# A two-layer model on eight cores: rows of the light FFN turned by DMA in the first stage, and q and k projected ahead of it in the first block

## The chip, the cores and the metric

The kernel runs on one Trainium2 chip, on all 8 cores. Each core computes one batch element on its own; the cores exchange no data. A time is the device time in microseconds (us) of the slowest of the eight cores. A profile shows one execution, on its slowest core (core 4 here), and times in it count from the start of the span.

## The reference

For one batch element x is 2048 tokens by 1024 channels. Two layers run in sequence, each `x = x + s * silu(f)` with an attention part s and a feed-forward part f of the normalised rows. The change touches only the start of the first layer:

```python
xn = _layernorm(x)                                   # rows of 1024 channels
x_proj = silu(xn @ W1 + b1); u, v, q, k = split(x_proj, 4)
scores = einsum('bqhd,bkhd->bhqk', qh, kh); attn = silu(scores) / S
y = _layernorm(attn_v * u) @ W2 + b2                 # attention part of layer 0
# feed-forward part of layer 0, on xn: rmsnorm, a light FFN for every row,
light = gelu(rmsnorm(xn) @ w1_l.T + b1_l) @ w2_l.T + b2_l
# and a heavy FFN for the 1024 rows with the highest scores xn . routing_token
```

Layer 1 is an attention with softmax and a gated FFN with 4096 hidden channels; its matmuls are most of the time.

## The kernel before

The program is written engine by engine: each helper appends an instruction to the list of one engine (`Q["t"]` TensorE, `Q["s"]` ScalarE, `Q["v"]` VectorE, `Q["g"]` POOL, `Q["y"]` SP), with waits on counters between them. Each engine runs its list in order, so the order in which the Python code calls the helpers is the order on each engine. DMAs are issued by SP (`y_dma`) or by POOL (`g_dma`); SP's waits stand in SP's list like any other entry, so a DMA is not issued before the waits of all DMAs ahead of it are met.

The first stage runs over 16 tiles of 128 rows (tile `tt`), in 4 blocks of 4 tiles (block `bl` holds tiles 4 bl to 4 bl + 3). It loads a tile of x (`xt0`, six buffers, lines 257 to 263) and then does this:

- `stats(bl)` (line 335): VectorE computes mean and variance of the four tiles (lines 343 to 346), ScalarE one square root, VectorE a few 128x4 operations, the last of them at line 363.
- `scale_rows(tt)` (line 365): `xnb`, the rows normalised for the attention (by ScalarE at line 373 for the first four tiles, by POOL at line 378 for the rest; two buffers), and `xrb`, the rows normalised for the FFN (POOL, line 383; four buffers). SP stores xrb to `xrsp` in HBM, for the later gather of the heavy rows.
- `turn_rows(tt, ...)` (line 390): TensorE turns xnb (eight 128x128 transposes into a PSUM bank, line 398) and VectorE copies the bank to `xn` (line 402); TensorE turns xrb (line 409) and ScalarE copies that bank to `xrT` (line 413); VectorE multiplies the rows with the routing token `rtb`, which is loaded once, and sums them (line 419); then SP loads the tile six further on.
- `light1(bl, m)` (line 425): the first matmul group of the light FFN, four groups of eight 128x512 matmuls on `xrT` and `w1l`, and a gelu on ScalarE. xrT has one buffer for a block; a new block writes it after light1 of the block before. `w1l` is made once by VectorE from the loaded `w1lf` (`fold_w1l`, line 280).
- `proj_uqk` (line 284) and `proj_v2` (line 302): projections q, k, u (eight 128x512 matmuls each) and v (two groups) of the block, with silu on ScalarE.

In the loop over the blocks, `stats` of the next block and `scale_rows` of its first two tiles come first; then light1 of this block, then q, k, u, v, v, and behind each of the first four of these one tile of the next block is turned. When the stage is done on TensorE, POOL issues the load of the next projection weights (`ld_wu[1]`), and the attention of layer 0 begins.

Of the kernel before, what the change touches and what calls it, by code (L numbers as in the profile page):

```python
# [17 lines left out]
NCH = 8  # L18
# [13 lines left out]
def build_program():  # L32
# [75 lines left out]
    Q = {"t": [], "s": [], "v": [], "g": [], "y": []}  # L108
# [40 lines left out]
    def SI(emit): return _inc("s", cs, emit)  # L149
# [32 lines left out]
    vrs = lambda nm, a, b: VROW[0:1, VR[nm] + a:VR[nm] + b]  # L182
# [6 lines left out]
    eye_bf = small("eye_bf", [128, 128], BF16)  # L189
# [67 lines left out]
    def load_x0(tt):  # L257
        if tt < NTT:
            sl = tt % NX
            if x0_free[sl] is not None:  # L260
                wk("y", *x0_free[sl])
            x0_ld[tt] = y_dma(qx0[sl], xt0[sl][:], xtok[tt * 128:(tt + 1) * 128, :])
    for tt in range(4):
        load_x0(tt)
    k_rt = y_dma(stream("qrt"), rtb[:], vrs("rt", 0, 1024).partition_broadcast(128))
    w1lv = w1lT.rearrange("(c p) n -> p c n", p=128)
    qw1l = [stream("qw1l0"), stream("qw1l1")]
    ld_w1l = [y_dma(qw1l[0], w1lf[0][:], w1lv[:, 0:4, :])]
    for tt in range(4, NX):
        load_x0(tt)  # L270
    ld_w1l.append(y_dma(qw1l[1], w1lf[1][:], w1lv[:, 4:8, :]))

    wk("g", x0_ld[3])
    ld_wu[0] = g_dma(qwu[0], wuqk[0][:], Wuqk[0, :, :, :])
# [115 lines left out]
    def turn_rows(tt, k_n, k_r, st):  # L390

        sl = tt % NX
        s2 = tt % 2
        s4 = tt % 4
        b = take()
        wk("t", k_n)
        for c in range(NCH):
            (TN if c < NCH - 1 else TI)(lambda t, c=c, b=b, s2=s2: t.transpose(
                pbh(b)[:, c * 128:(c + 1) * 128], xnb[s2][:, c * 128:(c + 1) * 128], eye_bf[:]))
        xnb_free[s2] = tok(ct)  # L400
        wk("v", tok(ct))
        VI(lambda v, tt=tt, b=b: v.tensor_copy(
            xn[:, :, tt * 128:(tt + 1) * 128], pbh(b).rearrange("p (c n) -> p c n", c=NCH)))
        give(b, tok(cv))
        k_xn[tt // 4] = tok(cv)
        b = take()
        wk("t", k_r)
        for c in range(NCH):
            (TN if c < NCH - 1 else TI)(lambda t, c=c, b=b, s4=s4: t.transpose(
                pbh(b)[:, c * 128:(c + 1) * 128], xrb[s4][:, c * 128:(c + 1) * 128], eye_bf[:]))  # L410
        xrb_free[s4] = (tok(ct), st)
        wk("s", tok(ct), xrT_free[0])
        SI(lambda s, tt=tt, b=b: s.copy(
            xrT[:, :, (tt % 4) * 128:(tt % 4 + 1) * 128], pbh(b).rearrange("p (c n) -> p c n", c=NCH)))
        give(b, tok(cs))
        k_xr[tt // 4] = tok(cs)
        wk("v", k_rt)
        VD()
        k_s = VI(lambda v, tt=tt, sl=sl: v.scalar_tensor_tensor(
            sjunk[:], xt0[sl][:], mv[:, tt, 0:1], rtb[:], OP.subtract, OP.mult,  # L420
            accum_out=c16["sraw"][:, tt:tt + 1]))
        x0_free[sl] = (k_n, k_r, k_s)
        load_x0(tt + NX)
# [22 lines left out]
    for bl in range(NTG):  # L446
        if bl + 1 < NTG:
            stats(bl + 1)
            for tt in range(4 * bl + 4, 4 * bl + 6):
                rows[tt] = scale_rows(tt)  # L450
        wk("t", k_xr[bl], k_w1l)
        for m in range(4):
            light1(bl, m)
        xrT_free[0] = tok(ct)
        wk("t", k_xn[bl])
        parts = [lambda nm=nm: proj_uqk(0, nm, bl) for nm in "qku"]
        parts += [lambda tp=tp: proj_v2(0, tp) for tp in (2 * bl, 2 * bl + 1)]
# [1457 lines left out]
```

How the kernel before makes its waits and increments, by code:

```python
    def dma(q, st, out, in_):  # L110
        st.n += 16
        Q[q].append(lambda e, o=out, i=in_, h=st.h: e.dma_start(out=o, in_=i).then_inc(h, 16))
        return (st, st.n)
# [4 lines left out]
    def y_words(st, out, in_):  # L118
        st.n += 16
        Q["y"].append(lambda e, o=out, i=in_, h=st.h: e.dma_start(
            out=o, in_=i, allow_slow_non_contiguous=True).then_inc(h, 16))
        return (st, st.n)
# [4 lines left out]
    def wt(q, ctr, v):  # L128
        if v > 0:
            Q[q].append(lambda e, h=ctr.h, vv=v: e.wait_ge(h, vv))
# [13 lines left out]
    def _inc(q, ctr, emit):  # L144
        ctr.n += 1
        Q[q].append(lambda e, f=emit: f(e).then_inc(ctr.h, 1))
        return (ctr, ctr.n)
# [347 lines left out]
    def routing():  # L495
# [84 lines left out]
            w2_sum(j)  # L580
        k_accW[0] = tok(cv)
        wk("v", k)
        VI(lambda v: v.tensor_scalar(hdi[:], desti[:], NHEAVY, None, OP.min))
        wk("g", k)
        qtab = stream("qtab")
        for tt in range(NTT):
            qtab.n += 16
            Q["g"].append(lambda g, tt=tt: g.indirect_dma_start(
                tab_d, bass.IndirectOffsetOnAxis(desti[:, tt:tt + 1], 0), tokid[:, tt:tt + 1], None
                ).then_inc(qtab.h, 16))
        k_rows = tok(cv)
        wk("y", tok(qtab))
        k = y_words(stream("qr10"), sidx[:], tab_d[0:NHEAVY, :].rearrange("(t p) o -> p (t o)", p=128))
# [6 lines left out]
            Q["g"].append(lambda g, st=st: g.indirect_dma_start(  # L600
                xrg[st][:], None, xrsp, bass.IndirectOffsetOnAxis(sidx[:, st:st + 1], 0)
                ).then_inc(qxg.h, 16))
        k_gather[0] = tok(qxg)
```

## Time and profile before

| what | value |
|---|---|
| median of 3 runs (lowest to highest) | 4214.24 us (4206.66 to 4214.62) |
| profiled execution, its own time | 4205.8 us |
| its span on the slowest core (core 4) | 4204.2 us |
| spans of the other cores | 4160.4 to 4195.4 us |
| TensorE matmuls, busy | 3919.9 us (93%) |
| ScalarE, busy | 2097.0 us (50%) |
| VectorE, busy | 1634.2 us (39%) |
| POOL, busy | 413.6 us (10%) |

The profiled execution is one run, 8.4 us under the median of the three timed ones. Busy shares are means over the whole span; the change touches the first 127.5 us alone, where the shares are others. Each row of a timeline is one instruction or several alike in a row: its start, its time, its engine, its line in the program, what it writes and reads, and in brackets how long the engine was idle before it and what ended that.

### The profile page before, as it was taken

How to read it: one execution, taken by the hardware profiler on the slowest of the kernel's cores; microseconds unless marked ns; L12 is line 12 of the kernel's file. 1: busy time of each engine (PE TensorE's matmuls, PEld its weight loads, DVE VectorE, ACT ScalarE, POOL GpSimd, SP SyncE). 2: the span in 40 equal slices, each digit the busy share in tenths (PEclk: the TensorE clock that was granted, in tenths of full speed). 3: DMA queues.
4: the chain of work that ended last, by engine and by line, in shares of the span. 5: the costliest groups of instructions: out<-in, count | busy, mean ns of one | idle time of the engine just before them, and what ended most of it. 6: DMA issues, size and time to landing. Idle time of an engine off the chain costs nothing.

```text
span 4204.2 us, 55884 instructions; the slowest of 8 cores (4160.4 to 4204.2 us)
## 1 busy us (share of the span) xinstructions
PE 3919.9 (93%) x20362; PEld 1681.0 (40%) x20362; DVE 1634.2 (39%) x1775; ACT 2097.0 (50%) x2027; POOL 413.6 (10%) x684
## 2 busy tenths in 40 slices
PE   6799777799899999999999999999999999999999
PEld 3333232344444433344443344444344434433444
DVE  6485411002563435333244434424453342355421
ACT  4799757620450556443355554525654553467101
POOL 3000110101110000001100000020000002100000
PEclk9999988999899999999999999999999999999999
DMA  5466865845443349998433333343333334333794
GB/s 157 79 106 109 120 96 105 126 74 152 144 159 128 130 127 220 218 218 212 144 126 123 112 132 117 137 152 113 122 131 124 122 122 145 133 115 119 230 302 143
DMA packets 146591, 593.24 MB, mean 141 GB/s; under 512 B 22517, under 2 KB 49429, under 8 KB 102677
## 3 DMA queue, kind: packets, MB, share of 16 engines
q0 software_dynamic: 80960, 448.84, 41.5%
q1 hardware_dynamic: 65370, 140.83, 10.3%
q8 instruction: 174, 2.85, 0.3%
q14 instruction: 87, 0.71, 0.1%
HBM read 637.80 MB, written 120.63 MB: 180 GB/s over the span
## 4 chain that ended last, share of the span: by engine, by line
PE 76%; DMA 8%; ACT 8%; issue 4%; DVE 3%; DVEq 2%; POOL 0%; SPq 0%; ACTq 0%; POOLq 0%
PE psP L1697 37%; PE psP L1663 10%; PE psP L1719 5%; ACT pt L786 4%; PE psP L1465 3%; PE psP L1413 3%; PE psP L929 3%; PE psP L987 3%; PE psP L1291 2%; DMA w2s<-W 2%; PE psP L291 2%; DVEq L153 1%; PE psP L779 1%; PE psP L312 1%; DMA wsl<-h2wt 1%
## 5 line engine op out<-in xcount | busy, mean ns | idle before, releaser
L1697 PE MATMUL psP<-hB,wsl 128*128 128x512 bf16 x4096 | 923.3, 382 | 23.1 <-DMA wsl<-h2wt 14.2
L1697 PE MATMUL psP<-hA,wsl 128*128 128x512 bf16 x4096 | 928.8, 381 | 3.7 <-DVE nrm L1337 3.7
L1489 DVE TENSOR_TENSOR accs<-accs,pt 128x2048 f32<-128x2048 f32 x192 | 440.1, 2292 | 897.7 <-ACT pt L1480 897.6
L1697 PEld LDWEIGHTS psP<-hB,wsl 128*128 128x128 bf16 x4096 | 393.9, 98 | 524.5 <-issue 77.4
L1697 PEld LDWEIGHTS psP<-hA,wsl 128*128 128x128 bf16 x4096 | 389.4, 98 | 509.3 <-issue 67.8
L1480 ACT ACTIVATE pt<-psP,nbias 128x1024 bf16<-128x1024 f32 x512 | 542.6, 1111 | 93.6 <-PE psP L1465 86.7
L786 ACT ACTIVATE pt<-psP 128x2048 bf16<-128x2048 f32 x341 | 476.6, 1449 | 80.2 <-PE psP L779 76.4
L1663 PE MATMUL psP<-xn,wsl 128*128 128x512 bf16 x2048 | 452.0, 379 | 3.5 <-ACT sgt L1139 1.8
L1480 ACT ACT_TABLE_LOAD x200 | 256.6, 1283 | 355.8 <-PE psP L1465 338.0
L1704 ACT ACT_TABLE_LOAD x181 | 232.2, 1283 | 259.9 <-PE psP L1697 257.1
L1663 PEld LDWEIGHTS psP<-xn,wsl 128*128 128x128 bf16 x2048 | 199.1, 98 | 242.1 <-issue 7.6
L1704 ACT ACTIVATE hA<-psP,vcol 128x512 bf16<-128x512 f32 x128 | 88.0, 687 | 334.9 <-PE psP L1697 334.0
L1719 PE MATMUL psP<-hA,wsl 128*128 128x512 bf16 x1024 | 234.4, 386 | 6.2 <-DMA wsl<-w3wt 6.2
L779 PE MATMUL psP<-q_p,k_p 64*128 64x512 bf16 x1024 | 175.9, 394 | 61.2 <-ACT pt L786 59.7
L1671 ACT ACTIVATE t1f<-psP,vcol 128x512 f32<-128x512 f32 x128 | 88.0, 687 | 271.9 <-PE psP L1663 268.4
L1677 DVE SCALAR_TENSOR_TENSOR hA<-psP,vcol,t1f 128x512 bf16<-128x512 f32 x128 | 96.1, 751 | 326.4 <-PE psP L1663 292.9
L759 PE MATMUL psP<-pt,v 128*64 128x512 bf16 x1024 | 155.4, 405 | 53.6 <-DVE au L766 51.0
L291 PE MATMUL psP<-xn,wuqk 128*128 128x512 bf16 x768 | 186.1, 387 | 7.3 <-DMA wuqk<-Wuqk 6.7
L1465 PE MATMUL psP<-q_p,k_p 64*128 64x512 bf16 x1024 | 156.9, 385 | 20.9 <-ACT pt L1480 19.9
L112 POOL DMA_DIRECT2D wsl<-h1b x125 | 66.4, 531 | 1078.8 <-PE psP L1697 850.3
L1704 ACT ACTIVATE hB<-psP,vcol 128x512 bf16<-128x512 f32 x128 | 88.0, 687 | 167.8 <-PE psP L1697 166.5
L1413 PE MATMUL psP<-pt,v_p 128*64 128x512 bf16 x1024 | 160.1, 393 | 0.3 <-DVE cxf L1423 0.3
(229 smaller groups left out, 3243.1 us busy)
## 6 DMA issues: line engine op xcount, KB each, us to landing
wsl<-h1b POOLq DMA_DIRECT2D x125, 1024.0 KB, 5.1
wsl<-h2b POOLq DMA_DIRECT2D x96, 1024.0 KB, 5.1
h1b<-h1wt POOLq DMA_DIRECT2D x32, 1024.0 KB, 11.1
wsl<-h2wt POOLq DMA_DIRECT2D x32, 1024.0 KB, 13.7
h2b<-wsl SPq DMA_DIRECT2D x32, 1024.0 KB, 13.3
wsl<-w1b POOLq DMA_DIRECT2D x96, 256.0 KB, 3.6
wsl<-w2b POOLq DMA_DIRECT2D x96, 256.0 KB, 4.1
wsl<-w3b POOLq DMA_DIRECT2D x24, 1024.0 KB, 5.3
```

The lines of the kernel that those rows point to most:

```text
L291: (TN if c < NCH - 1 else TI)(lambda t, c=c, g=g, b=b, p=p, j=j: t.matmul(pb(b), wuqk[p % 2][:, c, j * 128:(j + 1) * 128], xn[:, c, g * 51 ...
L759: (TI if h == 1 else TN)(lambda t, p=p, tk=tk, sl=sl, col=col, h=h: t.matmul(psP[64 * h:64 * h + 64, 6, :], v2[(p // 2) % 2][:, tk, (p % 2 ...
L779: (TI if (i == len(ents) - 1 and h == 1) else TN)(lambda t, p=p, g=g, tk=tk, i=i, h=h: t.matmul(pb(base + 2 * i + h), k_p[p % 2][64 * h:64 ...
L786: SI(lambda s, sl=sl, n=n, base=base, o=o: s.activation(pt[sl][:, o:o + n * 1024], psP[:, base:base + 2 * n, :], AF.Silu))
L1413: emitter(lambda t, p=p, tk=tk, sl=sl, tkk=tkk, h=h: t.matmul(psP[64 * h:64 * h + 64, 4, :], v_p2[p % 3][:, tk, 64 * h:64 * h + 64], pt2[s ...
L1465: emitter(lambda t, p=p, tk=tk, g=g, h=h, tkk=tkk: t.matmul(pb(2 * h + tkk), k_p2[p % 2][64 * h:64 * h + 64, tk * 128:(tk + 1) * 128], q_p ...
L1480: emitter(lambda s, p=p, sl=sl, h=h: s.activation(pt2[sl][:, h * 1024:(h + 1) * 1024], psP[:, 2 * h:2 * h + 2, :], AF.Exp, bias=nbias[p % ...
L1489: VI(lambda v, a=a, sl=sl: v.tensor_tensor(accs[:], a[:], pt2[sl][:], OP.add))
L1663: emitter(lambda t, i=i, c=c, o=hh * 16 + m * 8 + c, b=b, Qs=Qs: t.matmul(pb(b), wsl[i][:, o, :], xn[:, c, Qs], start=(c == 0), stop=(c == ...
L1697: emitter(lambda t, it=it, i=i, b=b, src=src: t.matmul(pb(b), wsl[i][:, it, :], src[:, it, :], start=(it == 0), stop=(it == 31)))
L1704: SI(lambda s, ot=ot, b=b, dst=dst, nm=nm: s.activation(dst[:, ot, :], pb(b), AF.Gelu, scale=vcs(nm, ot)))
L1719: emitter(lambda t, it=it, i=i, b=b: t.matmul(pb(b), wsl[i][:, it, :], hA[:, it, :], start=(it == 0), stop=(it == 31)))
```

## The change

Three things change. The load of `rtb` goes from the place behind the first four tiles of x to the end of the first loads, and the two halves of `w1lf` take turns with tiles 4 and 5. The turn of `xrb` is no longer made by TensorE and ScalarE but by one DMA on SP's queue, from SBUF to SBUF, transposing 128x1024 into the block's columns of `xrT`. And in the first block the projections of q and k stand ahead of light1; the list of parts that takes turns with the tiles of the next block is then shorter by two (u, v, v, and two empty places).

```diff
+    def y_turn(st, out, in_):
+
+        st.n += 16
+        Q["y"].append(lambda e, o=out, i=in_, h=st.h: e.dma_start(out=o, in_=i, transpose=True).then_inc(h, 16))
+        return (st, st.n)
...
-    k_rt = y_dma(stream("qrt"), rtb[:], vrs("rt", 0, 1024).partition_broadcast(128))
     w1lv = w1lT.rearrange("(c p) n -> p c n", p=128)
     qw1l = [stream("qw1l0"), stream("qw1l1")]
-    ld_w1l = [y_dma(qw1l[0], w1lf[0][:], w1lv[:, 0:4, :])]
-    for tt in range(4, NX):
-        load_x0(tt)
-    ld_w1l.append(y_dma(qw1l[1], w1lf[1][:], w1lv[:, 4:8, :]))
+    ld_w1l = []
+    for h in range(2):
+        ld_w1l.append(y_dma(qw1l[h], w1lf[h][:], w1lv[:, 4 * h:4 * h + 4, :]))
+        load_x0(4 + h)
+    k_rt = y_dma(stream("qrt"), rtb[:], vrs("rt", 0, 1024).partition_broadcast(128))
...
+    qxrT = [stream(f"qxrT{i}") for i in range(4)]
...
-        b = take()
-        wk("t", k_r)
-        for c in range(NCH):
-            (TN if c < NCH - 1 else TI)(lambda t, c=c, b=b, s4=s4: t.transpose(
-                pbh(b)[:, c * 128:(c + 1) * 128], xrb[s4][:, c * 128:(c + 1) * 128], eye_bf[:]))
-        xrb_free[s4] = (tok(ct), st)
-        wk("s", tok(ct), xrT_free[0])
-        SI(lambda s, tt=tt, b=b: s.copy(
-            xrT[:, :, (tt % 4) * 128:(tt % 4 + 1) * 128], pbh(b).rearrange("p (c n) -> p c n", c=NCH)))
-        give(b, tok(cs))
-        k_xr[tt // 4] = tok(cs)
+        wk("y", xrT_free[0])
+        k = y_turn(qxrT[s4], xrT[:, :, (tt % 4) * 128:(tt % 4 + 1) * 128], xrb[s4][:])
+        xrb_free[s4] = (k, st)
+        k_xr.setdefault(tt // 4, []).append(k)
...
-        wk("t", k_xr[bl], k_w1l)
+        wk("t", k_xn[bl])
+        first_two = "qk" if bl == 0 else ""
+        for nm in first_two:
+            proj_uqk(0, nm, bl)
+        wk("t", *k_xr[bl], k_w1l)
         for m in range(4):
             light1(bl, m)
         xrT_free[0] = tok(ct)
-        wk("t", k_xn[bl])
-        parts = [lambda nm=nm: proj_uqk(0, nm, bl) for nm in "qku"]
+        parts = [lambda nm=nm: proj_uqk(0, nm, bl) for nm in "qku" if nm not in first_two]
         parts += [lambda tp=tp: proj_v2(0, tp) for tp in (2 * bl, 2 * bl + 1)]
-        for i, f in enumerate(parts):
-            f()
+        for i in range(5):
+            if i < len(parts):
+                parts[i]()
```

SP, the first loads (xt is a tile of x, w1lf a half of the light weights before folding), as one piece of the difference from the kernel before (-) to the changed one (+):

```order
 L112 DMA xt_100<-xtok 128x1024
-L112 DMA rtb<-VROW 128x1024
 L112 DMA w1lf_105<-w1lT 128x4x512
 L112 DMA xt_101<-xtok 128x1024
+L112 DMA w1lf_106<-w1lT 128x4x512
 L112 DMA xt_102<-xtok 128x1024
-L112 DMA w1lf_106<-w1lT 128x4x512
+L112 DMA rtb<-VROW 128x1024
 L112 DMA xrsp<-xrb_111 128x1024 [waits cg]
```

rtb now stands behind 3 MB of loads that it stood ahead of. On VectorE the order is the same in both kernels. In the changed one's first block the pair of COPY (the copy to xn) and the multiplication with rtb (which waits for its load on qrt) stands four times, once for each tile, and behind the fourth come the folds of w1l (line 286) and the first statistics of block 1 (line 350):

```order
L409 COPY xn_179<-psP 128x8x128 [waits ct]
L419 SCALAR_TENSOR_TENSOR sjunk,c_sraw<-xt_100,mv,rtb 128x1024 [waits qrt]
L286 TENSOR_SCALAR w1l<-w1lf_105,vcol 128x512 [waits qw1l0]
L286 TENSOR_SCALAR w1l<-w1lf_105,vcol 128x512 x3
L286 TENSOR_SCALAR w1l<-w1lf_106,vcol 128x512 [waits qw1l1]
L286 TENSOR_SCALAR w1l<-w1lf_106,vcol 128x512 x3
L350 BN_STATS bns_50<-xt_101 128x6 [waits qx04]
```

All of these, and three of the four copies to xn, stand behind the first row that waits for qrt. On SP, from the end of block 0's part of the list to block 1's, the piece of the difference is:

```order
 L112 DMA xrsp<-xrb_113 128x1024 [waits cg]
+L128 DMA_TRANSPOSE xrT<-xrb_112 128x8x128 [waits ct]
 L112 DMA xt_102<-xtok 128x1024 [waits cg,cv]
 L112 DMA xrsp<-xrb_114 128x1024 [waits cg]
+L128 DMA_TRANSPOSE xrT<-xrb_113 128x8x128 [waits ct]
 L112 DMA xt_97<-xtok 128x1024 [waits cg,cv]
+L128 DMA_TRANSPOSE xrT<-xrb_114 128x8x128 [waits ct]
 L112 DMA xt_98<-xtok 128x1024 [waits cg,cv]
```

The transposes of a block's third and fourth tile (xrb_113, xrb_114) both stand behind the store of the fourth. In the last two turned blocks the loads of xt between them are absent. TensorE's list for the first block and the start of the next is, before (line 398 turns xnb, 409 xrb, 428 is light1, 291 q, k or u, 312 v):

```order
L428 MATMUL psP<-xrT,w1l 128x512 x32
L291 MATMUL psP<-xn_179,wuqk_81 128x512 x8
L398 MATMUL psP<-eye_bf,xnb_109 128x128 x8
L409 MATMUL psP<-eye_bf,xrb_111 128x128 x8
L291 MATMUL psP<-xn_179,wuqk_81 128x512 x8
L398 MATMUL psP<-eye_bf,xnb_110 128x128 x8
```

and in the changed kernel (line 405 turns xnb, 297 is q, k or u, 318 v):

```order
L297 MATMUL psP<-xn_179,wuqk_81 128x512 x16
L428 MATMUL psP<-xrT,w1l 128x512 x32
L297 MATMUL psP<-xn_179,wuqk_81 128x512 x8
L405 MATMUL psP<-eye_bf,xnb_109 128x128 x8
L311 MATMUL psP<-b1v_bf,ones_bf 128x512
L318 MATMUL psP<-wv_83,xn_179 128x256 x16
L405 MATMUL psP<-eye_bf,xnb_110 128x128 x8
```

q and k have moved ahead of light1, and the turns of xrb are gone from between the projections.

## Rows read from the trace of the kernel before

**Rows 1.** Busy time by stretch: us, each engine (instructions), granted clock, DMA share, GB/s

```profile
0.00:37.30 37.30, 5.75 (x64) 5.25 (x65) 20.98 (x52) 9.97 (x10) 6.82 (x12) 0.96 0.92 236
...
61.05:86.10 25.05, 20.80 (x156) 12.37 (x154) 16.58 (x34) 13.68 (x17) 12.33 (x8) 1.00 0.35 119
...
110.90:127.50 16.60, 16.57 (x92) 8.52 (x89) 0.00 (x0) 8.35 (x11) 0.00 (x0) 1.00 0.00 1
```

**Rows 2.** The chain of waits in order of time: start, us, what

```profile
7.61 27.68 DMA w1lf<-w1lT
...
128.04 8.44 DMA wuqk<-Wuqk
```

**Rows 3.** Tile rtb in the first stage: min/median/max ns, first and last start

```profile
L419 DVE SCALAR_TENSOR_TENSOR sjunk<-xt,mv,rtb x16: 1283/1578/2195, 25.1 to 109.3; 128x1024 bf16<-128x1024 f32 x16
...
L112 SPq DMA_DIRECT2D rtb<-VROW x1: 641/641/641, 4.6 to 4.6; - x1
...
DMA to landing us min/median/max: 12.9/12.9/12.9
```

**Rows 4.** Timeline of VectorE in the first block

```profile
27.22 0.68 DVE L402 COPY xn<-psP 128x1024 bf16<-128x1024 bf16 x1
...
33.18 1.67 DVE L280 TENSOR_SCALAR w1l<-w1lf,vcol 128x512 bf16<-128x512 f32 x4
35.38 1.67 DVE L280 TENSOR_SCALAR w1l<-w1lf,vcol 128x512 bf16<-128x512 f32 x4 [0.54 <-DMA w1lf<-w1lT]
37.14 0.69 DVE L343 BATCH_NORM_STATS2 bns<-xt 128x6 f32<-128x512 f32 x1
```

**Rows 5.** Stretch of the first matmuls after the weight load: columns as in rows 1

```profile
136.60:140.10 3.50, 3.47 (x8) 1.00 (x8) 0.00 (x0) 0.00 (x0) 0.00 (x0) 0.54 1.02 205
```

**Rows 6.** Timeline, from the last tile turned in block 0 into block 1

```profile
56.13 2.16 POOL L383 TENSOR_SCALAR xrb<-xt,c_rr,c_nmrr 128x1024 bf16<-128x1024 f32 x1
...
57.73 0.61 PE L398 MATMUL psP<-eye_bf,xnb 128*128 128x128 bf16 x8
...
58.36 0.32 SPq L112 DMA_DIRECT2D xrsp<-xrb  x1
...
60.61 0.69 DVE L343 BATCH_NORM_STATS2 bns<-xt 128x6 f32<-128x512 f32 x1
...
61.05 7.07 PE L428 MATMUL psP<-xrT,w1l 128*128 128x512 bf16 x32
...
67.96 1.89 PE L291 MATMUL psP<-xn,wuqk 128*128 128x512 bf16 x8
```

**Rows 7.** Timeline of block 1: its first turn, and the last with what follows

```profile
72.36 0.61 PE L398 MATMUL psP<-eye_bf,xnb 128*128 128x128 bf16 x8 [2.51 <-POOL xnb L378]
...
81.03 1.92 PE L312 MATMUL psP<-wv,xn 128*128 128x256 bf16 x16
...
81.19 2.16 POOL L383 TENSOR_SCALAR xrb<-xt,c_rr,c_nmrr 128x1024 bf16<-128x1024 f32 x1
...
82.79 0.61 PE L398 MATMUL psP<-eye_bf,xnb 128*128 128x128 bf16 x8
...
85.67 0.70 DVE L343 BATCH_NORM_STATS2 bns<-xt 128x6 f32<-128x512 f32 x1
```

**Rows 8.** Timeline of the end of block 2 and the start of block 3

```profile
105.97 1.20 POOL L383 TENSOR_SCALAR xrb<-xt,c_rr,c_nmrr 128x1024 bf16<-128x1024 f32 x1
...
107.81 0.61 PE L398 MATMUL psP<-eye_bf,xnb 128*128 128x128 bf16 x8
...
110.88 7.07 PE L428 MATMUL psP<-xrT,w1l 128*128 128x512 bf16 x32
```

**Rows 9.** Tile xrsp in the first stage: issue to landing of its 16 stores

```profile
DMA to landing us min/median/max: 2.0/2.4/13.1
```

**Rows 10.** DMA issues of the whole span: KB each, median us to landing

```profile
xt<-xtok SPq DMA_DIRECT2D x16, 512.0 KB, 8.0
...
sgsp<-sgt POOLq DMA_DIRECT2D x16, 256.0 KB, 4.7
```

## The prediction

> **What bounds the kernel now.** I read first the stretches of the first stage, [rows 1]. The stage lasts 127.5 us of a span of 4204.2 us, and no engine fills it: in the first 37.3 us the DMA engines are busy 0.92 of the time and TensorE 5.75 us, and in a middle block of 25.05 us TensorE is busy 20.80, VectorE 16.58 and POOL 12.33. So the block is held by a chain that passes from engine to engine. The chain of waits, [rows 2], says where the stage begins and how it is tied to the rest: up to 35.3 us (7.61 + 27.68) it stands on the second half of w1l, and at 128.04 on a weight load that POOL may issue only when TensorE has finished the stage. Nothing behind the stage can start before that load, so what the stage gains or loses, the kernel gains or loses.
>
> Then I followed one block. VectorE makes the statistics of the next four row tiles, POOL makes two scaled copies of each, xnb and xrb, one after the other, TensorE turns xnb, VectorE copies it to xn and multiplies the rows with rtb, and only when the last of the four is through can the next statistics start. Removing the turns of xrb from TensorE and their copies from ScalarE shortens it only where TensorE came late for a turn of xnb. Block b below means the tiles 4b to 4b+3; light1(b) is the light FFN's first matmul group on them.
>
> **Part 1: rtb goes to the end of the first loads.** In the kernel before, the load of rtb is issued at 4.6 us and lands 12.9 us later, at 17.5 [rows 3]; the last load of this group lands at 35.3 [rows 2]. SP issues the same 5.5 MB in both kernels, only in another order, and the load issued first landed first. So I take rtb's landing, now the last, as 35.3. The first multiplication with rtb started at 25.1 [rows 3]. VectorE works in order, and behind that instruction stand the copies of tiles 1 to 3 to xn, the eight folds of w1l and the statistics of block 1. Before, VectorE reached the folds at 33.18 and waited for w1l until 35.38, so the late w1l cost it almost nothing; now this wait is taken 10 us earlier in the queue and the work behind it comes on top. From 35.4: one multiplication without POOL beside it, 1.28 [rows 3], puts the second copy at 36.7 instead of 27.22; the rounds from there to the first fold took 33.18 - 27.22 = 5.96 [rows 4], so folds start at 42.65; 1.70 for the first half and 37.14 - 35.38 = 1.76 for the second put the statistics of block 1 at 46.1 instead of 37.14. **Cost A: +9.0 us.** Loading w1l earlier gains nothing, since the folds are not reached.
>
> **Part 2: q and k ahead of light1(0).** They need the copy of tile 3, now done at 41.4 (36.7 + 2 x 1.99 + 0.7), take some 1.6 for a lowered clock (8 such matmuls took 3.47 us at a mean granted clock of 0.54 after a wait, so most of them at 1.2 GHz, not 2.4 [rows 5]) and 2 x 1.89 [rows 6]. They end at 46.8, beside the folds (46.05). light1(0) follows until 53.9, u until 55.8. The first turn of block 1 needs POOL's xnb, not before 56. So the move is free here, but it does not win back A.
>
> **Part 3: 16 turns of xrb and 16 copies leave TensorE and ScalarE.** A turn is eight matmuls, 0.61 us, after a wait for xrb. What counts is the last turn of xnb in a block. Tile 7's ran at 57.73, though its xnb was done by 56.13, where POOL starts the next copy [rows 6]: 1.6 us late. After, TensorE has nothing else ahead of it, so it runs at 56.13 + 9.0 = 65.1. **Gain B: -1.6.** Statistics of block 2: 60.61 + 9.0 - 1.6 = 68.0, 7.4 late. The copies on ScalarE hide beside its other work and free nothing; no wait in [rows 6, 7] is for a PSUM bank. Block 1 has the same 1.6 to give (turn at 82.79, xnb done by 81.19 [rows 7]), if TensorE is in time.
>
> **Part 4: 16 transposing DMAs on SP's queue.** The trace has no such DMA. Bounds for one, from issue to landing: 2.0 us, the fastest store of the same 256 KB from the same tile on the same queue, and 8.0, the median of the stage's loads, which sat behind other transfers [rows 9, 10]. I take 4.7, the median of the store of sgsp [rows 10]: also 256 KB, cut into 256-byte runs, as the turned rows are (128 tokens of 2 bytes). For SP's time to issue one: 0.32, its time for a store [rows 6], to 0.64, that for the broadcast [rows 3]; I take 0.64. Nobody waits for them inside a block, but light1 of the next block needs all four, and SP is in order: the transposes of a block's last two tiles both stand behind the store of the last tile, which waits for POOL's last xrb, and in the first two blocks a load of 512 KB stands between them.
>
> Block 0: POOL's last xrb ends at 56.13 + 2.16 + 9.0 = 67.3 [rows 6]. Store, transpose, load, transpose: the last is issued 1.4 later and lands at 73.4; light1(1), before at 61.05, starts there. 7.07 + 1.89 + 1.6 of clock [rows 5, 6] put the first turn of block 1's loop at 84.0, where POOL alone would allow 72.36 + 7.4 = 79.8 [rows 7]. From there to the last turn TensorE needs three turns, k, u and v (0.65 + 1.9 + 0.65 + 1.9 + 0.65 + 2.3 = 8.05, a v group being 1.92 and a bias matmul of 0.4): 92.0, while POOL would allow 81.19 + 7.4 = 88.6. So 92.0 - 82.79 = 9.2: the delay is back, and block 3's statistics start at 94.9 instead of 85.67. **Cost C: +1.8, from 7.4 to 9.2.**
>
> Block 1's last xrb ends at 83.35 + 7.4 = 90.75; store and one transpose ahead (1.0), landing at 96.5; light1(2) and q then end near 107, about when POOL delivers, so nothing is added. Block 2's last xrb ends at 105.97 + 1.20 + 9.2 = 116.4 [rows 8], its transposes land at 116.4 + 1.0 + 4.7 = 122.1, while TensorE is done with block 2 at 118.2 (last xnb 105.97 + 9.2, turn 0.65, v 2.3). light1(3) started at 110.88 [rows 8]: **11.2 us late, so cost D is +2.0** over 9.2. In the last block light1 stands ahead of everything, so this landing is exposed in full; up to 1.6 of clock may come after the 4 us of idle TensorE, of which I take half. The 16.60 us behind it [rows 1] do not change.
>
> **Sum:** 9.0 - 1.6 + 1.8 + 2.0 + 0.8 = 12.0 us. The profiled execution took 4205.8 us in all, 1.6 more than its span: 4217.8. The median of the runs is 8.4 above that execution (4214.24); on the median the forecast is 4226. With 2.0 and 0.32 for the transpose the same walk gives +5.2 (C vanishes to -1.2, D is 116.1 against 115.2 for TensorE itself); with 8.0 it gives C +5.1, D +5.3, all clock, +19.4.
>
> **Rivals.** *R1, rtb is not late.* Should the DMA engines serve rtb ahead of its turn, A goes. For it: its source is one row of 4 KB, read 128 times, and the 16 engines need not keep step. Against: before, 3 us between two issues became 18 between their landings [rows 2, 3], as in a queue that keeps its order. It decides at a landing of 25.1 us; each us later costs one. At 25.1 the sum is 12.0 - 9.0 = +3, 4217: not slower than can be told.
>
> *R2, the transposes are as quick as a plain store.* +5.2 to +6: 4220. For it: the DMA engines are free by then, the share is 0.35 and falling [rows 1]. Against: the run length. The Trainium skill states it outright (Advanced Engine Details and Errata, X-Bar Transpose (TRN2): a transposing DMA is as fast as a regular one); no run here shows it yet, and by it the sum would be the +5.2 just given.
>
> *R3, the transposes go one at a time and set the pace.* A block has four of them in 25.05 us [rows 1], so beyond 6.3 us each, one after the other, they take the place of the chain. At 8.0 each, 16 from 36.3 us (1 us behind rtb, after two stores) end at 164.3 instead of 110.88: +53, 4268. For it: all are on one in-order queue. Against: SP's own time for an issue is 0.32 to 0.64. The Trainium skill speaks for it (VectorE: DVE Perf Modes, The three transpose paths: 1309 ns by DMA for a block of 128x128, against 390 ns on TensorE). As an estimate from that page, eight blocks in a row are 10.5 us and the end comes at 204, some +94. On TensorE the trace disagrees with it, with 0.61 us for eight.
>
> *R4, the work taken off TensorE counts in full:* 16 x 0.61 = 9.8 us less, 4204. It needs TensorE as the bound, and [rows 1] shows it idle 4.25 of 25.05 us; even R1 and R2 together come to 5.2 - 9.0 = -3.8.
>
> **How the numbers follow.** Forecast (+8.4 to +20): 0.55. R3: 0.11. R2: 0.16. R1: 0.10. R4 and what I do not see: 0.08, of which 0.06 is faster. A measurement of this kernel can tell about 0.2%, 8.4 us. Slower: 0.55 + 0.11 = 0.66; within: 0.16 + 0.10 + 0.02 = 0.28; faster: 0.06. The range leaves out R3 and R4. Its top is 4214.2 + 19.4 and 4 for the runs' own spread; its foot is R1, 4217, less 6 for the same reason (the lowest run is 7.6 under the median).
>
> **What would show it.** A: VectorE idle from about 25 to 35, ended by rtb's landing, and the first statistics of block 1 near 46. If they start near 37, R1 holds. B: the last turn of block 0 right behind its xnb. C, D: TensorE waiting ahead of light1(1) and light1(3) for a DMA to xrT, with landings near 4.7; near 2, R2; SP idle on its own transposes, and landings far above 6, R3. The stage's last matmul near 139.5 instead of 127.5. The prediction is wrong above all if rtb lands early, or if VectorE has other work ahead of that wait.

## The result: slower by 0.3 to 0.6%, in the first stage

| | before | changed |
|---|---|---|
| median of all runs, first comparison | 4214.76 us | 4253.05 us |
| ratio, first comparison (95% interval) | | 1.0055 (1.0032 to 1.0077) |
| ratio, second comparison (95% interval) | | 1.0034 (1.0015 to 1.0052) |
| first attention scores, mean of the eight cores | 126.7 us | 143.3 us |
| first attention scores, core 4 | 129.0 us | 144.3 us |

Some executions of each kernel ran with one die or both at a lower clock; ratios, spans and marks below leave these out, so that the marks of e7 are those of cores 0 to 3, and those of e9 of cores 2 to 5, where the rows up to the mark are as fast as in the other kernels. The ratio of the first comparison is +23 us (13 to 32), that of the second +14 us (6 to 22); the forecast was +12. The direction held, and so did the path of the late rtb. The price of the transposing DMAs did not: it was too low by 10 us, and most of that is hidden in the sum. The size was too small by 3 us on the core that was walked through, and by more on most of the others.

The mark I use below is the start of the first attention scores, the first instruction that uses what the stage has made. It is read from one profile of each kernel. It is free of what attention adds: from the first scores of layer 0 to the last it takes 636 to 656 us on the cores before and 635 to 664 in the changed kernel. What the stage loses, the kernel loses: over the runs of the second comparison the mean of the eight core spans went from 4185.8 to 4202.6 us (+16.8), and the mark went up by 16.5.

**The profile after**, core 4 of the second profile of the changed kernel (span 4208.1 us), beside the rows of core 4 before. Tile rtb, which answers to [rows 3]:

```profile
L112 SPq DMA_DIRECT2D rtb<-VROW x1: 580/580/580, 9.8 to 9.8; - x1
...
DMA to landing us min/median/max: 23.3/23.3/23.3
```

It is issued at 9.8 instead of 4.6 us and lands at 33.1 instead of 17.5. VectorE's timeline, for [rows 4]:

```profile
33.18 1.28 DVE L419 SCALAR_TENSOR_TENSOR sjunk<-xt,mv,rtb 128x1024 bf16<-128x1024 f32 x1 [11.51 <-DMA rtb<-VROW]
...
34.39 0.69 DVE L409 COPY xn<-psP 128x1024 bf16<-128x1024 bf16 x1
...
40.35 3.25 DVE L286 TENSOR_SCALAR w1l<-w1lf,vcol 128x512 bf16<-128x512 f32 x8
43.70 0.69 DVE L350 BATCH_NORM_STATS2 bns<-xt 128x6 f32<-128x512 f32 x1
```

VectorE stands still for 11.51 us, and the first statistics of block 1 come at 43.70 instead of 37.14. SP's timeline of the same stretch shows what the prediction had left out, the transposing DMAs of block 0, and the last of block 1's:

```profile
21.01 9.98 SPq L128 DMA_TRANSPOSE xrT<-xrb  x1
34.55 0.34 SPq L112 DMA_DIRECT2D xt<-xtok  x1
34.98 0.39 SPq L112 DMA_DIRECT2D xrsp<-xrb  x1
35.41 1.49 SPq L128 DMA_TRANSPOSE xrT<-xrb  x1
...
38.18 1.73 SPq L128 DMA_TRANSPOSE xrT<-xrb  x1
...
40.69 3.16 SPq L128 DMA_TRANSPOSE xrT<-xrb  x1
...
65.71 1.50 SPq L128 DMA_TRANSPOSE xrT<-xrb  x1
...
68.31 1.88 SPq L128 DMA_TRANSPOSE xrT<-xrb  x1
```

The first one holds SP for 9.98 us, while the first loads are in flight (rtb lands at 33.1); the last of the block is issued at 40.69. TensorE's timeline, for [rows 6 to 8]:

```profile
39.31 5.75 PE L297 MATMUL psP<-xn,wuqk 128*128 128x512 bf16 x16 [15.22 <-DVE xn L409]
47.61 8.48 PE L428 MATMUL psP<-xrT,w1l 128*128 128x512 bf16 x32 [2.55 <-DMA xrT<-xrb]
...
57.66 0.61 PE L405 MATMUL psP<-eye_bf,xnb 128*128 128x128 bf16 x8
...
64.19 0.61 PE L405 MATMUL psP<-eye_bf,xnb 128*128 128x128 bf16 x8 [0.69 <-POOL xnb L385]
74.15 8.86 PE L428 MATMUL psP<-xrT,w1l 128*128 128x512 bf16 x32 [9.35 <-DMA xrT<-xrb]
...
84.57 0.61 PE L405 MATMUL psP<-eye_bf,xnb 128*128 128x128 bf16 x8
...
99.24 9.95 PE L428 MATMUL psP<-xrT,w1l 128*128 128x512 bf16 x32 [4.92 <-DMA xrT<-xrb]
...
124.49 8.75 PE L428 MATMUL psP<-xrT,w1l 128*128 128x512 bf16 x32 [3.99 <-DMA xrT<-xrb]
...
140.84 1.92 PE L318 MATMUL psP<-wv,xn 128*128 128x256 bf16 x16
```

All four light1 groups now wait for the DMA that turns xrb, 20.8 us together. The last three take 8.75 to 9.95 us instead of 7.07. The first, 8.48, is no slower than before, when it waited for w1l:

```profile
37.31 8.80 PE L428 MATMUL psP<-xrT,w1l 128*128 128x512 bf16 x32 [7.20 <-DVE w1l L280]
```

Busy time by stretch, one for each group, tells why they are slow (us, then each engine with its instructions, granted clock, DMA share, GB/s):

```profile
47.61:56.09 8.48, 8.48 (x33) 3.57 (x34) 3.60 (x15) 5.42 (x8) 3.58 (x4) 0.83 0.09 35
74.15:83.01 8.86, 8.86 (x33) 3.68 (x34) 1.89 (x11) 4.73 (x6) 4.22 (x4) 0.79 0.13 46
99.24:109.19 9.95, 9.95 (x33) 3.88 (x34) 2.76 (x13) 4.83 (x6) 4.68 (x4) 0.70 0.08 28
124.49:133.24 8.75, 8.75 (x33) 3.65 (x34) 0.00 (x0) 3.35 (x4) 0.00 (x0) 0.80 0.01 2
```

The granted clock is 0.70 to 0.83 over such a group, so part of it ran at 1.2 GHz and the rest at 2.4, after 2.55 to 9.35 us in which TensorE waited. The stage's last matmul ends at 142.8 (140.84 + 1.92), so its last stretch, from light1(3) on, takes 18.3 us where [rows 1] had 16.60.

### The profile page after: what moved, and what is told of

Read it like the earlier page. It is cut to its first block, busy times and chain, and to the rows that moved or that the text cites. A ratio compares the mean times of both kernels' runs of the same rounds, so it can differ in the third digit from the quotient of the medians.

```text
span 4330.9 us, 55593 instructions; the slowest of 8 cores (4214.7 to 4330.9 us)
## 1 busy us (share of the span) xinstructions
PE 4026.2 (93%) x20234; PEld 1696.9 (39%) x20234; DVE 1631.3 (38%) x1775; ACT 2084.1 (48%) x2012; POOL 414.0 (10%) x684
## 4 chain that ended last, share of the span: by engine, by line
PE 77%; DMA 8%; ACT 7%; issue 3%; DVE 2%; DVEq 1%; SPq 0%; POOL 0%; ACTq 0%; POOLq 0%
PE psP L1701 39%; PE psP L1667 10%; PE psP L1723 5%; ACT pt L790 4%; PE psP L1469 3%; PE psP L1417 3%; PE psP L933 3%; PE psP L991 3%; PE psP L1295 2%; DMA wsl<-h2wt 2%; DMA w2s<-W 2%; PE psP L297 2%; DMA h2b<-wsl 2%; PE psP L783 1%; PE psP L763 1%
## 5 line engine op out<-in xcount | busy, mean ns | idle before, releaser
L1701 PE MATMUL psP<-hB,wsl 128*128 128x512 bf16 x4096 | 970.3, 396 | 24.8 <-DMA wsl<-h2wt 20.7
L1701 PE MATMUL psP<-hA,wsl 128*128 128x512 bf16 x4096 | 973.9, 394 | 3.7 <-DVE nrm L1341 3.7
L1701 PEld LDWEIGHTS psP<-hB,wsl 128*128 128x128 bf16 x4096 | 405.0, 101 | 561.4 <-issue 233.8
L1701 PEld LDWEIGHTS psP<-hA,wsl 128*128 128x128 bf16 x4096 | 399.3, 100 | 544.4 <-issue 210.0
L1723 PE MATMUL psP<-hA,wsl 128*128 128x512 bf16 x1024 | 245.3, 399 | 6.8 <-DMA wsl<-w3wt 6.8
```

The source lines that it names most:

```text
L1701: emitter(lambda t, it=it, i=i, b=b, src=src: t.matmul(pb(b), wsl[i][:, it, :], src[:, it, :], start=(it == 0), stop=(it == 31)))
L1723: emitter(lambda t, it=it, i=i, b=b: t.matmul(pb(b), wsl[i][:, it, :], hA[:, it, :], start=(it == 0), stop=(it == 31)))
```

## The experiments

Theory 1, that of the prediction: the late rtb costs most (+9), the transposing DMAs +3 beside it. Theory 2: the transposing DMAs cost more than that by themselves. Theory 3: something behind the stage grows too. The first four kernels take the parts apart. In the tables "scores" is the mark named above, as a mean over the cores; "waits" is the sum of TensorE's waits for xrT on core 4 (core 0 for e6 and e7).

| kernel | scores, us | against before | waits, us | ratio to before (95% interval) |
|---|---|---|---|---|
| before | 126.7 | | | |
| e2: rtb late alone | 134.7 | +8.0 | 0 | 1.0014 (0.9992 to 1.0036) |
| e3: transposing DMAs alone | 141.0 | +14.3 | 36.3 | 1.0041 (1.0016 to 1.0067) |
| e1: all but the late rtb | 140.1 | +13.4 | 28.0 | 1.0029 (1.0004 to 1.0054) |
| e4: the changed kernel | 143.3 | +16.5 | 20.8 | 1.0034 (1.0015 to 1.0052) |

**e1, the first loads as before.**

```diff
+    k_rt = y_dma(stream("qrt"), rtb[:], vrs("rt", 0, 1024).partition_broadcast(128))
...
-    for h in range(2):
-        ld_w1l.append(y_dma(qw1l[h], w1lf[h][:], w1lv[:, 4 * h:4 * h + 4, :]))
-        load_x0(4 + h)
-    k_rt = y_dma(stream("qrt"), rtb[:], vrs("rt", 0, 1024).partition_broadcast(128))
+    ld_w1l = [y_dma(qw1l[0], w1lf[0][:], w1lv[:, 0:4, :])]
+    for tt in range(4, NX):
+        load_x0(tt)
+    ld_w1l.append(y_dma(qw1l[1], w1lf[1][:], w1lv[:, 4:8, :]))
```

> The changed kernel with rtb and the first loads in the order of the kernel before; the transposing DMAs and q, k first stay. Theory 1 (the late rtb costs 9 us through VectorE's order): statistics of block 1 start near 37 to 38 us instead of 43 to 46, attention's first scores come 8 to 10 us earlier than in the changed kernel (about 134 to 137 instead of 142 to 146), and the whole is +7 to +12 us against the kernel before (1.002 to 1.003). Rival (the order of loads does not matter, the transposes cost it all): first scores stay at 142 to 146 and the ratio stays near 1.0055.

The scores gain only 3.2 us on the changed kernel (140.1 against 143.3), less than theory 1 expected and more than its rival. VectorE and TensorE on core 4:

```profile
35.25 0.70 DVE L350 BATCH_NORM_STATS2 bns<-xt 128x6 f32<-128x512 f32 x1
...
44.76 9.71 PE L428 MATMUL psP<-xrT,w1l 128*128 128x512 bf16 x32 [9.94 <-DMA xrT<-xrb]
```

The statistics of block 1 are back at 35.25, but light1(0) starts at 44.76, after 9.94 us of waiting for xrT, where it started at 37.31 before. What the late rtb had cost is taken over by the transposing DMAs of block 0.

**e2, only the first loads changed** (the reverse of the diff above, on the kernel before).

> The kernel before with the new order of the first loads alone. Theory 1: VectorE idles some 10 us for rtb in block 0, statistics of block 1 start near 46 instead of 37, first scores come 8 to 9 us late (about 134 to 138 instead of 125 to 129), ratio 1.0015 to 1.0025. If what a late first stage costs grows in the attention behind it (theory 2), the ratio is above 1.003 with the same shift of the first scores. Rival (no cost): nothing moves.

+8.0 in the mean, +5.4 on core 4 (134.4 against 129.0); the ratio alone could not be told from 1. VectorE on core 4:

```profile
32.20 1.28 DVE L419 SCALAR_TENSOR_TENSOR sjunk<-xt,mv,rtb 128x1024 bf16<-128x1024 f32 x1 [11.23 <-DMA rtb<-VROW]
...
42.72 0.69 DVE L343 BATCH_NORM_STATS2 bns<-xt 128x6 f32<-128x512 f32 x1
```

VectorE waits 11.23 us for rtb, the statistics of block 1 start 5.6 us later than before (the expectation had them near 46), and the loss is passed on unchanged from block to block: light1(1) to light1(3) start at 66.67, 91.75 and 116.25, each 5.4 to 5.7 later than before and each at 7.07 us. So cost A is real, and its mechanism is the one forecast.

**e3, only the turn by DMA.**

```diff
-        b = take()
-        wk("t", k_r)
-        for c in range(NCH):
...
-        k_xr[tt // 4] = tok(cs)
+        wk("y", xrT_free[0])
+        k = y_turn(qxrT[s4], xrT[:, :, (tt % 4) * 128:(tt % 4 + 1) * 128], xrb[s4][:])
+        xrb_free[s4] = (k, st)
+        k_xr.setdefault(tt // 4, []).append(k)
```

> The kernel before with the transposing DMAs alone: old order of loads, light1 ahead of q and k in every block. Theory 1: each transpose holds SP 1.3 to 1.5 us and lands 3 to 7 us after its issue, so TensorE waits for xrT ahead of light1(1) to light1(3) by 4 to 10, 3 to 5 and 4 us, and first scores come 6 to 11 us late; ratio 1.0015 to 1.003. Rival (the turns taken off TensorE pay for it): first scores within 2 us of the kernel before, ratio 0.999 to 1.0005.

+14.3, nearly as much as the whole change, and more than the 6 to 11 that theory 1 allowed. VectorE's folds and TensorE on core 4:

```profile
29.43 3.25 DVE L286 TENSOR_SCALAR w1l<-w1lf,vcol 128x512 bf16<-128x512 f32 x8
...
42.47 9.89 PE L428 MATMUL psP<-xrT,w1l 128*128 128x512 bf16 x32 [18.82 <-DMA xrT<-xrb]
71.38 9.09 PE L428 MATMUL psP<-xrT,w1l 128*128 128x512 bf16 x32 [7.72 <-DMA xrT<-xrb]
97.50 9.68 PE L428 MATMUL psP<-xrT,w1l 128*128 128x512 bf16 x32 [5.72 <-DMA xrT<-xrb]
122.52 8.75 PE L428 MATMUL psP<-xrT,w1l 128*128 128x512 bf16 x32 [4.04 <-DMA xrT<-xrb]
```

VectorE had its folds done at 32.7, so light1(0) waits 18.82 us for nothing but xrT, a wait that no expectation had named, and the delay of 11.6 us over the kernel before stands at light1(3) as it stood at light1(2) (11.4). Theory 2 holds. The parts don't add: 8.0 + 13.4 = 21.4 against 16.5, since in block 0 VectorE's wait for rtb and TensorE's wait for xrT run side by side.

**e4, the changed kernel unaltered**, beside the others on the same chip.

> The changed kernel once more beside the three others, for a trace of it at full clock. Theory 1 (all is lost in the first stage and passed on one to one): first scores 14 to 20 us late on each core, the last scores and the end of the span late by the same, ratio 1.0035 to 1.005. Theory 2 (the attention behind it gets longer too): the last scores are late by 10 us or more beyond the first, ratio 1.0055 to 1.008.

+16.5 at the scores (12.9 to 19.2 on single cores), +16.8 in the mean of the spans. The length of the attention behind the mark is 645.2 us in the mean before and 646.7 to 652.5 in these four kernels, with the cores of one run 20 to 29 us apart, so by itself it settles little. The spans do: their mean over the cores goes up by 14.3 (e1), 8.5 (e2), 16.3 (e3) and 16.8 us (e4), the mark by 13.4, 8.0, 14.3 and 16.5. At most 2.0 us are left for what lies behind, and theory 3 is not needed.

The next four ask what in the DMAs costs: their place in the queue, light1 standing first, or the transposition itself.

| kernel | scores, us | against before | waits, us | ratio to before (95% interval) |
|---|---|---|---|---|
| e5: light1 last in its block | 132.9 | +6.2 | 0 | - |
| e6: the same, folds later | 132.5 | +5.8 | 0 | - |
| e7: transposing DMA ahead of the store (cores 0 to 3) | 132.9 | +6.3 | 20.1 | 1.0029 (1.0014 to 1.0044) |
| e8: q and k first, nothing else | 125.6 | -1.1 | 2.1 | - |

A dash stands where there were too few runs for a ratio.

**e5 and e6, light1 behind the v groups** (e5: the kernel before, with the turn by DMA; `turn_block` issues the four transposing DMAs of a block together, once light1 has freed xrT):

```diff
-        wk("t", k_xr[bl], k_w1l)
-        for m in range(4):
-            light1(bl, m)
...
         for i, f in enumerate(parts):
             f()
...
+        wk("t", *k_xr[bl], k_w1l)
+        for m in range(4):
+            light1(bl, m)
+        xrT_free[0] = tok(ct)
+        if bl + 1 < NTG:
+            turn_block(bl + 1)
```

> Transposing DMAs kept, rtb early as in the kernel before; light1 of a block stands behind its q, k, u, v, v, and the four transposes of the next block are issued together behind the loads of x, when light1 has freed xrT. Theory 1 (the transposes cost what TensorE waits for them ahead of light1, and the lower clock behind each wait): TensorE no longer waits for a DMA to xrT, light1 takes 7.1 us again, and first scores fall from 138 to 143 back to 123 to 129, the kernel before or up to 5 us better; ratio 0.999 to 1.0005. Rival (transposes slow the stage by their traffic or by holding SP, wherever light1 stands): first scores stay above 135, ratio above 1.002.

e6 has in addition the w1l loads behind tiles 4 and 5 and the folds behind the statistics of block 1.

> As e5_light1_last, and with light1 no longer early, the two halves of w1l are loaded behind tiles 4 and 5 and folded behind the statistics of block 1. Theory 1 (VectorE's order sets the stage): statistics of block 1 start near 33 instead of 37, first scores 3 to 5 us ahead of e5; ratio 0.998 to 1.000. Rival (tiles 6 and 7 land too late for it): the statistics stop at tile 6, first scores as in e5.

The wait is gone, as theory 1 of e5 had it, but the scores stay between its range and its rival's; e6 gains 0.4 us, as good as nothing, as its rival had it. In both, TensorE waits for xrT nowhere and on core 0 all four groups take 7.07 us. TensorE on core 0 of e6, the end of the stage:

```profile
106.65 1.92 PE L317 MATMUL psP<-wv,xn 128*128 128x256 bf16 x16
108.41 7.07 PE L428 MATMUL psP<-xrT,w1l 128*128 128x512 bf16 x32
115.32 5.34 PE L296 MATMUL psP<-xn,wuqk 128*128 128x512 bf16 x24
...
124.83 7.07 PE L428 MATMUL psP<-xrT,w1l 128*128 128x512 bf16 x32
```

So the transposition as such takes nothing from other engines that shows: the chain of VectorE and POOL ends even 0.6 us ahead of before (VectorE's last operation on `sraw`, the row sums of the stage, at 107.5 against 108.1, mean of the cores). The +5.8 that stay are an order of work: the light1 of two blocks, 14 us, now lies behind the turn of the last tile, where before there was that of one. On core 0 the stretch from there on is 7.0 us longer and starts 1.4 us earlier.

**e7, the transposing DMA ahead of its tile's store** (on e1):

```diff
-        wk("y", k_r)
-        st = y_dma(qxr[s4], xrsp[tt * 128:(tt + 1) * 128, :], xrb[s4][:])
...
-        wk("y", xrT_free[0])
+        wk("y", k_r, xrT_free[0])
         k = y_turn(qxrT[s4], xrT[:, :, (tt % 4) * 128:(tt % 4 + 1) * 128], xrb[s4][:])
+        st = y_dma(qxr[s4], xrsp[tt * 128:(tt + 1) * 128, :], xrb[s4][:])
```

> As e1_rtb_early, but each transpose stands ahead of its tile's store to HBM, and so the third tile's transpose is no longer behind the fourth tile's store. Theory 1 (SP's order and its 1.3 us an issue make a part of the wait): the wait ahead of light1(3) falls from 4.0 to 2 to 2.5 us, light1(0) starts earlier since the stores no longer stand ahead; first scores 2 to 5 us ahead of e1's 138 to 142. Rival (the wait is the landing alone): no change.

TensorE on core 0, the first and the last light1:

```profile
42.35 8.87 PE L427 MATMUL psP<-xrT,w1l 128*128 128x512 bf16 x32 [5.76 <-DMA xrT<-xrb]
...
115.34 7.07 PE L427 MATMUL psP<-xrT,w1l 128*128 128x512 bf16 x32 [2.18 <-DMA xrT<-xrb]
```

Seven of e1's 13.5 us on these cores are gone, more than the 2 to 5 expected, though SP is still held in block 0 (8.44 us on core 0). The time of the slowest core does not show it, with the ratio where e1 had it; the mean of the core spans does, +6.9 us where e1 had +14.3. With the store inside `scale_rows` as in e1, a block's second transposing DMA stands behind the store of its third tile and the third behind that of the fourth, and these wait for POOL's later xrb. That place in the queue, not the transfer, made half of e1's cost.

**e8, q and k ahead of light1(0), on the kernel before:**

```diff
+        first_two = "qk" if bl == 0 else ""
+        for nm in first_two:
+            proj_uqk(0, nm, bl)
         wk("t", k_xr[bl], k_w1l)
```

> The kernel before with q and k ahead of light1 in the first block alone. Theory 1: q and k fill the 7 us in which TensorE waited for w1l, but VectorE's and POOL's chain sets the block, so first scores move by less than 2 us; ratio 0.9995 to 1.0005. Rival (TensorE's time counts): first scores 4 to 5 us earlier.

-1.1 us, as e1 against e3 (-1.0), with single cores from 5.5 earlier to 3.2 later, so it can hardly be told from nothing, at which the prediction had put it. On core 4 the eight-matmul groups run from 28.93, in the wait for the folds. But the order lays light1(1) bare: on every core TensorE is there early and waits 1.7 to 2.1 us for ScalarE's last copy to xrT, and on six of eight the group is slower for it.

```profile
56.76 9.57 PE L428 MATMUL psP<-xrT,w1l 128*128 128x512 bf16 x31 [2.05 <-ACT xrT L413]
```

The last two ask whether block 0 is the larger half, and whether order alone can undo the rest.

**e9, block 0 turned on TensorE, blocks 1 to 3 by DMA** (on e1):

```diff
+        if tt < 4:
+            b = take()
+            wk("t", k_r)
...
+            k_xr.setdefault(0, []).append(tok(cs))
+        else:
+            wk("y", xrT_free[0])
+            k = y_turn(qxrT[s4], xrT[:, :, (tt % 4) * 128:(tt % 4 + 1) * 128], xrb[s4][:])
```

> As the kernel with the transposing DMAs and the old order of loads (first attention scores, mean over the cores, at 140.1 us, 13.4 behind the kernel before), but the four turns of xrb of the first block are made on TensorE and copied by ScalarE as before, so that no transposing DMA stands behind the full first loads. Theory (the first block's transposes cost most, because the first of them holds SP for 8 us at a full queue): light1(0) starts at 36 to 38 us again, at 7 to 9 us for its 32 matmuls, the first turn of its loop near 47, and the first scores near 133, 6 to 7 behind before; the waits for xrT ahead of light1(1) to light1(3) stay at 9, 5 and 4 us. Rival (each block costs its own wait, wherever it is): first scores at 137 to 138, only light1(0)'s lost clock saved.

Scores on cores 2 to 5 at 135.1, +8.3 on the same cores before (126.8), where e1 has +12.7. Ratio 1.003 (1.0017 to 1.0042). TensorE on core 5:

```profile
36.88 7.07 PE L441 MATMUL psP<-xrT,w1l 128*128 128x512 bf16 x32 [1.83 <-DVE w1l L286]
66.39 9.52 PE L441 MATMUL psP<-xrT,w1l 128*128 128x512 bf16 x32 [9.94 <-DMA xrT<-xrb]
91.69 8.75 PE L441 MATMUL psP<-xrT,w1l 128*128 128x512 bf16 x32 [4.47 <-DMA xrT<-xrb]
116.46 8.39 PE L441 MATMUL psP<-xrT,w1l 128*128 128x512 bf16 x32 [4.71 <-DMA xrT<-xrb]
```

Block 0 is worth 4.4 of the 12.7 us, the other three blocks together 8.3; both the theory (6 to 7 left) and the rival (10 to 11 left) were off, the theory by less. No transposing DMA held SP for more than 2.44 us on these cores.

**e10, e9 with the DMA ahead of the store and light1 behind q, k and u** (in block 3 behind v too). The edit moves two more things: in block 0 light1 stands first again, and in the blocks 1 and 2 all four tiles of the next block are turned behind light1:

```diff
+        if bl == 0:
+            jobs = [light, jobs[0], t4[0], jobs[1], t4[1], jobs[2], t4[2], vs[0], t4[3], vs[1]]
+        elif bl + 1 < NTG:
+            jobs = jobs + [light, t4[0], vs[0], t4[1], vs[1], t4[2], t4[3]]
+        else:
+            jobs = jobs + vs + [light]
```

> As the one above, with two more edits: in the blocks 1 to 3 each transposing DMA is issued ahead of its tile's store, and light1 stands behind q, k and u of its block (in the last block behind the v groups too), so that TensorE has 5.3 us of work, in the last block 9.9, before it needs xrT. Theory (the cost is the wait of light1 and the place of the transposes in SP's queue, not the transposition): no wait for xrT over 2.5 us in the blocks 1 to 3, all light1 groups but the first at 7.1 us, first scores at 124 to 127 (mean; before 126.7), and a time within 3 us of the kernel before, by the medians. Rival (a transposing DMA costs time wherever it stands, through SP, the DMA engines or VectorE's loads): first scores at 130 or later although TensorE waits for no xrT.

TensorE on core 4:

```profile
64.70 7.07 PE L444 MATMUL psP<-xrT,w1l 128*128 128x512 bf16 x31 [1.49 <-DMA xrT<-xrb]
71.60 0.61 PE L407 MATMUL psP<-eye_bf,xnb 128*128 128x128 bf16 x8
...
87.67 7.07 PE L444 MATMUL psP<-xrT,w1l 128*128 128x512 bf16 x31
...
115.80 6.85 PE L444 MATMUL psP<-xrT,w1l 128*128 128x512 bf16 x31
```

Scores at 123.6, 3.1 ahead of before, and the mean of the spans 2.2 ahead (4183.6 against 4185.8); ratio 0.9999 (0.9986 to 1.0012), so the whole time can't be told from before. The twelve DMAs that cost 8 us in e9 are still there; only the order around them differs (how much of it is the store's place, how much light1's and how much the turns', this kernel doesn't part). The theory held, with the scores 0.4 us ahead of its range; its rival fell. Without turns of xrb and with hardly a wait the stage is shorter, by less than the time can show.

## Why the prediction was right, and where it was wrong

**Step by step on core 4**, forecast against the rows above. rtb's landing, taken as 35.3: 33.1, in the order of the queue as assumed, 2.2 earlier. Statistics of block 1: forecast 46.1, measured 43.70, so A is +6.6 and not +9.0; that is the 2.2, and 0.2 of the multiplications and folds. q and k took 5.75 us instead of 3.78, near the forecast's 1.6 on top; the granted clock reads 1.00 there, so that it was the clock isn't shown. light1(0), forecast to start at 46.8 right behind q and k: 47.61, after 2.55 us of waiting for xrT. The last turn of block 0, B: forecast at 65.1 right behind POOL's xnb, measured 64.19 behind POOL's xnb; statistics of block 2 forecast 68.0, measured 68.38, since what A gave back the slow light1(0) took. light1(1), C: forecast 73.4, measured 74.15; first turn behind it 84.0, measured 84.57; statistics of block 3 94.9, measured 94.42. The prediction's tie of stage and kernel holds, though "nothing behind the stage can start before that load" was too strong: on core 4 before, the first scores started at 129.0, while the load issued at 128.04 took 8.44 us [rows 2]; they too stand behind the stage's last matmul.

At light1(1) two misses cancel. POOL's last xrb ahead of it ended at 65.2, where the forecast had 67.3, and xrT was there 8.9 us later instead of 6.1: the last two transposing DMAs took SP 1.50 and 1.88 us (the rows of SP above) instead of 0.64 each, and the last landed 5.8 us after its issue instead of 4.7.

```profile
64.03 1.20 POOL L390 TENSOR_SCALAR xrb<-xt,c_rr,c_nmrr 128x1024 bf16<-128x1024 f32 x1
```

**The step that failed** is light1(2), "so nothing is added". The walk put the first turn of block 1's loop at 84.0, 4.2 us behind what POOL would allow, and yet let POOL's last xrb of that block end only 7.4 us late, at 90.75. POOL has two buffers for xnb, and waits for that turn:

```profile
85.36 1.20 POOL L385 TENSOR_SCALAR xnb<-xt,c_rstd,c_nmr 128x1024 bf16<-128x1024 f32 x1 [1.84 <-PE psP L405]
...
90.83 2.16 POOL L390 TENSOR_SCALAR xrb<-xt,c_rr,c_nmrr 128x1024 bf16<-128x1024 f32 x1
```

The xrb ended at 93.0. So light1(2) waits 4.92 us, starts at 99.24 instead of 96.5 and takes 9.95, and the next turn, behind q, starts at 110.76 where the walk had 107. POOL waits for it in the same way:

```profile
111.54 1.20 POOL L385 TENSOR_SCALAR xnb<-xt,c_rstd,c_nmr 128x1024 bf16<-128x1024 f32 x1 [2.30 <-PE psP L405]
...
117.00 2.16 POOL L390 TENSOR_SCALAR xrb<-xt,c_rr,c_nmrr 128x1024 bf16<-128x1024 f32 x1
```

The last xrb of block 2 starts 11.0 us later than in [rows 8], not 9.2 (+1.8), and takes 2.16 instead of 1.20 (+0.96); a multiplication of VectorE had begun 0.35 us ahead of it (at 116.65), where before one began 0.28 us behind it (106.25). light1(3) follows 5.33 us behind its end, forecast 5.7 (-0.37), and the clock costs 1.7 in the last stretch, forecast 0.8 (+0.9). Together 1.8 + 0.96 - 0.37 + 0.9 = 3.3: the stage's last matmul at 142.8 instead of the forecast 139.5. The lowered clock was in the forecast, with 1.6 us at q and k, at light1(1) and in the 107 behind light1(2), and half of it at light1(3); over 7.07, the groups measured +1.4, +1.8, +2.9 and +1.7.

**The core.** Core 4 was the slowest core before, with its w1l landing last: its light1(0) started at 37.3, those of the others at 33.2 to 36.6. With the late rtb alone (e2) the first scores lie at 134.1 to 135.5 on all cores, where they lay at 124.8 to 129.1 before: all wait for a load that comes late on each, and the early cores lose their lead. In the changed kernel five of the other seven lose more than core 4, up to 19.2 us (core 6), and the mean is 16.5. A walk on the slowest core alone missed that, and which core is slowest in the end is not settled in this stage (core 2 in this profile, with the earliest scores of all).

**What agreed by luck.** By the forecast's parts, the change without the late rtb is worth +3 (its rival R1). e1 measured +13.4. So the price of the transposing DMAs was wrong by 10.4 us in the mean of the cores. Of these, 4.9 don't show, because in block 0 the wait for them runs beside the wait for rtb (8.0 + 13.4 against 16.5); 1.0 was paid back by the late rtb, which cost 8.0 and not 9.0; and 4.5 do show, 16.5 against 12. The prediction had light1(0) follow q and k at once, and so took the four DMAs of block 0 at nothing. They stand behind 5.5 MB of first loads, and the first of them holds SP for 10 us. The assumed 0.64 us of SP for one is 1.5 in the median here. Block 0 isn't all of it: without its DMAs, e9 still lost 8.3.

**The rivals.** R1 fell, rtb came as late as the order of the queue says. R2 fell: in tile xrT's answer the landing is 3.1 us at least and 4.5 in the median, against 2.0 and 2.4 for the store in [rows 9], and the changed kernel's own stores have 3.0 in the median over the stage. The Trainium skill (Advanced Engine Details and Errata, X-Bar Transpose (TRN2)) has the two alike; here the trace does not agree. R3 fell: two issued one behind the other took SP 3.4 us (at 93.46), and the row of tile xrT (ns, min/median/max, first and last start) shows one in 1.5:

```profile
L128 SPq DMA_TRANSPOSE xrT<-xrb x16: 1277/1492/9985, 21.0 to 121.0; - x16
...
DMA to landing us min/median/max: 3.1/4.5/14.4
```

Eight blocks of 128x128 in 1.5 us of issue and 4.5 to landing is also far from the 10.5 that the Trainium skill's figure made (VectorE: DVE Perf Modes, The three transpose paths). R4 fell in the changed kernel: TensorE lost 9.8 us of work and gained 20.8 of waiting for xrT. Only in e10 does some of it come back.

**Open.** Why the first transposing DMA holds SP for 7 to 10 us while the first loads are in flight, where a plain store there does not, was not taken apart. Nor were e10's edits, one from the other. The two comparisons, +23 and +14 us, have intervals that overlap.

## What to carry to other kernels

When work moves from an engine to a DMA, price it by where it will stand: what lies ahead of it on the issuing queue (stores that wait for the same producer, the first loads), and how much other work its reader has before it needs the result. The same twelve DMAs cost 8 us in e9, with light1 first and each DMA behind its store, and nothing in e10, with q, k and u first and each DMA ahead of it. Two waits in one stretch hide each other, so a sum that comes out right does not show that its terms are: run each part alone. A buffer that is freed late stops the engine that fills it, so carry a delay back to the producer before walking the next block. And walk the stage on an early core as well as on the slowest, for a load that comes late for all costs the early ones most.

## What the runs showed of the hardware that was not expected

- A transposing DMA of 256 KB from SBUF to SBUF takes SP 1.2 to 1.6 us for the issue in the median of a core, against 0.32 for a store of the same size [rows 6], and lands 3.0 to 3.2 us after it at best.
- The first one, issued at 19 to 22 us while the first loads were in flight, held SP for 6.7 to 10.0 us on each core read of e1, e3, e4 and e7; in the kernel before, two plain stores issued there (at 22.77) took 1.50 together. The twelve of e9 and e10, issued from 44 us on, took 2.54 us at most.
- With no wait ahead of it, light1's 32 matmuls took 7.07 us. Behind the waits of 3.99 to 18.82 us in the rows above they took 8.39 to 9.95, at a granted clock of 0.70 to 0.80 where it was read. Shorter waits went both ways: 7.07 behind 1.49 (e10), 2.18 (e7) and 3.61 us (e4, core 6), but 8.48 behind 2.55 (e4, core 4) and 8.6 to 9.7 behind 1.67 to 2.05 (light1(1) of e8, six cores).
